# Moving a transpose, its eviction and the bias work to other places in the first stage of a three-stage graph network kernel

## The chip, the core and the metric

The kernel runs on one core of a Trainium2 chip. The metric is the device time of one execution in microseconds (us). Three executions of the kernel before took 1197.25, 1198.56 and 1198.85 us; the median is 1198.56.

## The reference, cut to what matters

Sixteen graphs ("batches" below) of 512 nodes with 128 features go through two layers. The first layer, which the change touches, is this:

```
def _gat(h, adj, W, a):                       # used twice, W1 a1 and W2 a2
    Wh = h @ W
    e = leaky_relu(Wh @ a[:128] + swapaxes(Wh @ a[128:], 1, 2), 0.2)
    att = softmax(where(adj > 0, e, -9e15), axis=1)
    return att @ Wh
h = layernorm(x + gat(gat(x)))                # "first norm"
x = layernorm(h + relu(h @ w_ff1 + b_ff1) @ w_ff2 + b_ff2)      # "second norm"
```

The second layer is attention with 8 heads whose values depend on the relation code of each edge (values `src @ Wv[r] + bv[r]`, r = 0 to 3), a norm, a feed-forward part and a norm. Its biases `bv` are what the bias work prepares.

## The kernel before, in words

The kernel has three stages: the graph layer (`graph_layer`, tiles named `a_...`, about the first 420 us), the attention (`b_...`) and the last feed-forward part (`c_...`). All sixteen inputs stay on the chip between them, in `xs` and `codes`.

A batch has 4 chunks (C) of 128 nodes (P) and is worked on in four successive steps. Step t, run by `step(t, begin, first, second, feed, more)` on each engine, does four things at once for four different batches:

- **begin**, batch t: transposes the features (`turn_x`, L499) into the PSUM bank `turn`, ScalarE copies them to `x_t` (L701), the adjacency codes are transposed (`turn_codes`, L531) and copied to `codes` (L708), `x_weights` multiplies by the weights (L541), and the first attention's row is spread (`spread_row(0, t)`, L555).
- **first**, batch t-1: the scores of the first attention. ScalarE makes `low` from the row (`lower`, L822), VectorE adds and leaks (L863, "leak") and masks with a minimum (L870, "mask"; the mask itself is made by `edges`, L1027), ScalarE takes exponentials (`exps`, L841), VectorE the reciprocal of the sums (`invert`, L897) and scales (L904), TensorE multiplies (`round_one`, L593), ScalarE copies the result (`keep_hw`, L809).
- **second**, batch t-2: the same for the second attention: `spread_row(1, ...)`, `lower`, leaks, masks, `exps`, `invert`. GpSimd scales by the reciprocal (`scale_hw`, L1064, writes `hw_n`), TensorE multiplies (`round_two`, L583), VectorE adds the input (`add_x`, L1040) and does the first norm: `norm_stats(0)` (L914 and L921), ScalarE's root `rstds(0)` (L847 and L854, a logarithm and an exponential), `norm_finish` (L928, four scalings).
- **feed**, batch t-3: TensorE transposes the normed features (`turn_h`, L506), ScalarE evicts them (`keep_h`, L802), then `feed_up` (L567), `hidden` on ScalarE (L835), `feed_down` (L573), `add_h` (L1033), `turn_y` (L513), the second norm `norm_stats(1)`, `rstds(1)`, `norm_shift` (L935, "shift"), `centre` (L829, four chunks on ScalarE), and `turn_n` (L519), which turns the normed batch back, and `keep_x` (L815), which writes it to `xs`.

Steps 0 to 3 are unrolled, steps 4 to 14 are a hardware loop, step 15 and a hand-written `tail` follow. The order on each engine is written out by hand in its `step` function, and each engine works strictly in that order, waiting on semaphores. `step` of TensorE is L597, of ScalarE L693, of VectorE L953, of GpSimd L1048. In a step GpSimd does two things: `scale_hw` and then `encode` (L461, four instructions at L467), which makes the codes of batch t+1 once VectorE's `see` (L943) has looked at the codes of batch t-1. In step 3 it also writes pads (`first_qk.pads`, L255 to L257).

The order of the row transposes, `turn_n` and `turn_x` at the joint of two steps on TensorE is, before the change, `spread_row(0, t)`, `turn_n(t - 3)`, `spread_row(1, t - 1)`, `turn_x(t + 1)`, `turn_h(t - 2)`. On ScalarE it is `exps`, `rstds(1)`, `centre`, `keep_hw`, `rstds(0)`, the copy of `s2` (L739), `keep_x`, then of the next step `lower(1)`, the copy of `x_t`, `lower(0)`, `keep_h`.

`keep_x` and `centre` have these waits:

```
def keep_x(b):
    act.wait_ge(n_turned, b + 1)
    act.wait_ge(summed[0], b + 1)
def centre(b):
    act.wait_ge(shift_ready, b + 1)
    act.wait_ge(n_turned, b)
```

`Preparation.vector_late` (L161) is called at the end of VectorE's step 1. It forms differences of the value weights and of the biases (3 rows of 512), and splits the biases into three bf16 parts, one to a row, in fourteen chained instructions and a last cast. Its scratch space is lent by `hid` and `y`. Ahead of it it waits for all late loads (`late_loaded`), for which every engine also waits ahead of step 2. The only user of the result, `first_qk.values`, is in the tail.

Of the kernel before, what the change touches and what calls it, by code (L numbers as in the profile page):

```python
# [49 lines left out]
class Preparation:  # L50
# [3 lines left out]
    def __init__(self, nc, z, w, io, keep, sb, banks, lent):  # L54
# [11 lines left out]
        self.rest, self.acc, self.part, self.part2 = [at[0:3, 0:NB] for at in lent]  # L66
# [94 lines left out]
    def vector_late(self, dve):  # L161

        D, R, w = self.z.D, self.z.R, self.w
        rows, rest, part, part2, acc = self.rows, self.rest, self.part, self.part2, self.acc
        count = [0]

        def then(ins):

            count[0] += 1
            ins.then_inc(self.chain, 1)  # L170
            dve.wait_ge(self.chain, count[0])

        dve.wait_ge(self.late_loaded, 16 * len(self.late_loads))
        dve.wait_ge(self.ident_made, 4)

        for r in range(1, R):
            then(dve.tensor_tensor(w["wv"][:, r, :], w["wv"][:, r, :], w["wv"][:, 0, :], ALU.subtract))
            then(dve.tensor_tensor(rows[:, r * D:(r + 1) * D], rows[:, r * D:(r + 1) * D],
                                   rows[:, 0:D], ALU.subtract))

        e = w["ident"]
        then(dve.tensor_copy(part[:, :], rows[:, :]))
        then(dve.tensor_tensor(rest[:, :], rows[:, :], part[:, :], ALU.subtract))
        then(dve.tensor_scalar(acc[:, :], part[:, :], e[0:3, 0:1], None, ALU.mult))
        then(dve.tensor_copy(part[:, :], rest[:, :]))
        then(dve.tensor_tensor(part2[:, :], rest[:, :], part[:, :], ALU.subtract))
        then(dve.scalar_tensor_tensor(out=acc[:, :], in0=part[:, :], scalar=e[0:3, 1:2], in1=acc[:, :],
                                      op0=ALU.mult, op1=ALU.add))
        then(dve.scalar_tensor_tensor(out=acc[:, :], in0=part2[:, :], scalar=e[0:3, 2:3], in1=acc[:, :],
                                      op0=ALU.mult, op1=ALU.add))  # L190
        dve.wait_ge(self.ident_made, 5)
        dve.tensor_copy(w["bias3"][0:3, :], acc[:, :]).then_inc(self.biases_split, 1)
# [166 lines left out]
def graph_layer(nc, z, w, io, xs, codes, other, general, flagged, shared, first_qk, sem_b, keep):  # L359
# [5 lines left out]
    with ExitStack() as ctx:  # L365
# [125 lines left out]
        def _(pe):  # L491
# [105 lines left out]
            def step(t, begin, first, second, feed, more):  # L597
                if second:
                    spread_row(1, t - 2)
# [1281 lines left out]
```

## Time and profile before

| | us |
|---|---|
| runs | 1197.25, 1198.56, 1198.85 |
| median | 1198.56 |
| profiled execution | 1198.38 |
| its span in the trace | 1196.6 |
| TensorE busy (matmuls) | 1076.5 (90%) |
| VectorE busy | 948.1 (79%) |
| ScalarE busy | 741.5 (62%) |
| GpSimd busy | 602.8 (50%) |

The span is from the first to the last instruction; 1.8 us of the profiled execution lie around it. The profile names the engines PE (TensorE), PEld (its weight loads), DVE (VectorE), ACT (ScalarE), POOL (GpSimd) and SP. A row of a timeline has the start and the duration in us, the engine, the line, the operation, what it writes and reads, and how many instructions were merged into the row; an end in brackets says how long the engine stood idle ahead of it and what released it. Where instructions overlap in the engine's pipeline, one starts a little before the one ahead has ended, and a merged row's duration is that of all of them. The granted clock is a share of TensorE's full 2.4 GHz; 0.50 is its lower level, 1.2 GHz.

### The profile page before, as it was taken

The page shows a single profiled execution, that of the slowest core. Times are in us where ns is not written, and L with a number is a line of the kernel's source. Part 1 is how long each engine was busy: PE and PEld are TensorE (multiplying, and loading weights), DVE is VectorE, ACT ScalarE, POOL GpSimd, SP SyncE. Part 2 cuts the span into 40 slices and gives each one's busy share as a digit, 9 for nine tenths or more (in the row PEclk, how much of TensorE's full clock was granted, in tenths as well). Part 3 has the DMA queues.
Part 4 walks back from the last instruction along what each step waited for, and adds up shares of the span by engine and source line. Part 5 has one row for each costly group of instructions (what it writes and reads, how often), then busy time and mean ns, then how long its engine had stood idle before and what let it go on. Part 6 is the DMA issues. An engine that isn't in the chain of part 4 may idle for free. (4 is left out here: it accounts for less than half of the span.)

```text
span 1196.6 us, 21640 instructions
## 1 busy us (share of the span) xinstructions
PE 1076.5 (90%) x6087; PEld 496.7 (42%) x6087; DVE 948.1 (79%) x2324; ACT 741.5 (62%) x1341; POOL 602.8 (50%) x513
## 2 busy tenths in 40 slices
PE   3488888988988779999999999999999999879996
PEld 3465665665664422323333233333333323234442
DVE  2878878878888758888888888888888888437777
ACT  3467778778777346666666666676666666544442
POOL 3231231231211158788788887888788877900000
PEclk8699999999999979999999999999999999989998
DMA  5312112112104143223321433134313420000000
GB/s 163 108 54 106 53 53 105 53 54 104 53 11 120 40 118 91 63 79 116 111 60 60 114 110 79 40 114 114 84 46 99 114 62 1 1 0 36 35 35 35
DMA packets 49545, 86.54 MB, mean 72 GB/s; under 512 B 8919, under 2 KB 35927, under 8 KB 44378
## 3 DMA queue, kind: packets, MB, share of 16 engines
q1 hardware_dynamic: 46586, 85.59, 23.3%
q10 hardware_dynamic: 2912, 0.40, 0.2%
q8 instruction: 20, 0.33, 0.1%
q14 instruction: 27, 0.22, 0.1%
HBM read 52.12 MB, written 29.36 MB: 68 GB/s over the span
## 5 line engine op out<-in xcount | busy, mean ns | idle before, releaser
L1489 DVE TENSOR_REDUCE top<-b_peak 128x1 f32<-128x512 f32 x488 | 327.8, 687 | 89.4 <-PE b_peak L1245 85.2
L1360 ACT ACTIVATE b_prob<-b_score 128x1024 f32<-128x1024 f32 x256 | 262.1, 1024 | 199.1 <-PE b_score L1260 197.2
L1622 POOL TENSOR_TENSOR b_picked<-b_prob,mask 128x512 f32<-128x512 f32 x192 | 236.2, 1257 | 61.7 <-ACT b_prob L1360 61.6
L1622 POOL TENSOR_TENSOR b_picked<-b_prob,b_mask 128x512 f32<-128x512 f32 x192 | 237.3, 1263 | 53.6 <-ACT b_prob L1360 53.6
L1064 POOL TENSOR_TENSOR a_hw_n<-a_hw,a_inv 128x512 f32<-128x512 f32 x16 | 16.7, 1041 | 211.8 <-DVE a_inv L897 198.9
L467 POOL TENSOR_SCALAR a_code<-a_adj_in 128x512 bf16<-128x512 int32 x64 | 72.0, 1125 | 82.9 <-DVE a_seen L943 55.0
L841 ACT ACTIVATE a_att<-a_att,a_least 128x512 f32<-128x512 f32 x128 | 90.9, 714 | 16.4 <-DVE a_least L870 16.4
L1245 PE MATMUL b_peak<-b_k_stack,b_q_stack 96*128 96x512 bf16 x256 | 98.3, 384 | 0.0
L1245 PE MATMUL b_peak<-shared 96*128 96x512 bf16 x232 | 89.9, 389 | 6.0 <-issue 6.0
L870 DVE CUSTOM_DVE_ANT_0 a_att<-a_att,a_no_edge 128x512 f32<-128x512 f32 x128 | 94.7, 758 | 0.0
L1739 ACT ACTIVATE c_hid<-c_mid,bff 128x512 f32<-128x512 f32 x64 | 44.0, 687 | 62.5 <-PE c_mid L1717 62.5
L1260 PE MATMUL b_score<-shared 98*128 98x512 bf16 x256 | 77.6, 384 | 0.0
L1260 PE MATMUL b_score<-b_q_stack,b_k_stack 98*128 98x512 bf16 x256 | 76.5, 380 | 0.0
L573 PE MATMUL a_out<-a_hid,wff 128*128 128x512 f32 x128 | 59.5, 605 | 18.5 <-ACT a_hid L835 18.5
L1286 PE MATMUL b_o_ps<-b_picked,b_dval 128*32 128x512 f32 x512 | 68.2, 604 | 7.7 <-DVE b_picked L1503 5.2
L583 PE MATMUL a_turn<-a_hw_n,a_att 128*128 128x128 f32 x512 | 62.7, 282 | 13.5 <-POOL a_hw_n L1064 13.5
L1286 PE MATMUL b_o_ps<-b_picked,dval 128*32 128x512 f32 x512 | 68.2, 604 | 5.0 <-DVE b_picked L1503 5.0
L583 PEld LDWEIGHTS a_turn<-a_hw_n,a_att 128*128 128x128 f32 x512 | 60.3, 197 | 25.4 <-issue 25.4
L1245 PEld LDWEIGHTS b_peak<-b_k_stack,b_q_stack 96*128 96x128 bf16 x256 | 24.6, 96 | 108.7 <-DVE top L1489 93.8
L1286 PE MATMUL b_o_ps<-b_prob,b_val 128*32 128x512 f32 x512 | 68.2, 604 | 0.3 <-ACT b_o_t L1371 0.3
L1286 PE MATMUL b_o_ps<-b_prob,val 128*32 128x512 f32 x512 | 68.2, 605 | 0.0
L593 PE MATMUL a_pair<-a_xw_n,a_att 128*128 128x130 f32 x512 | 62.4, 281 | 4.8 <-DVE a_xw_n L904 4.8
(216 smaller groups left out, 1952.3 us busy)
## 6 DMA issues: line engine op xcount, KB each, us to landing
a_adj_in<-in_adj SPq DMA_DIRECT2D x16, 1024.0 KB, 5.5
scratch<-shared SPq DMA_DIRECT2D x32, 384.0 KB, 2.7
shared<-scratch SPq DMA_DIRECT2D x16, 768.0 KB, 6.3
scratch<-shared SPq DMA_DIRECT2D x32, 256.0 KB, 3.0
b_q_stack<-scratch SPq DMA_DIRECT2D x8, 768.0 KB, 5.4
b_k_stack<-scratch SPq DMA_DIRECT2D x8, 768.0 KB, 8.1
a_x_in<-in_x SPq DMA_DIRECT2D x16, 256.0 KB, 2.6
xs<-in_x SPq DMA_DIRECT2D x16, 256.0 KB, 5.6
```

The source lines that it names most:

```text
L467: eng.tensor_scalar(code[:, c, :].rearrange("p (k q) -> p k q", k=C), adj_in[:, c, :].rearrange("p (q k) -> p k q", k=C), CODE_HI, CODE_LO ...
L573: mm = pe.matmul(out[:, :], w["wff2"][0][:, f, :], hid[:, f, :], start=(f == 0), stop=(f == FC - 1))
L583: mm = pe.matmul(turn[:, ic * D:(ic + 1) * D], att[1][:, jc, ic * P:(ic + 1) * P], hw_n[:, jc, :], start=(jc == 0), stop=(jc == C - 1))
L593: mm = pe.matmul(pair[:, ic // 2, at:at + D + 2], att[0][:, jc, ic * P:(ic + 1) * P], xw_n[:, jc, :], start=(jc == 0), stop=(jc == C - 1))
L841: act.activation(att[k][:, c, :], att[k][:, c, :], ACT.Exp, bias=least[k][:, c:c + 1], scale=-1.0, accum_out=total[k][:, c:c + 1]).then_in ...
L870: dve.tensor_tensor_reduce(att[k][:, c, :], att[k][:, c, :], no_edge[:, c, :], 1.0, HIGHEST, ALU.add, ALU.min, least[k][:, c:c + 1]).then_ ...
L1245: pe.matmul(peak[hh % 2][:, :], q_stack[par][0:K, h, c * P:(c + 1) * P], k_stack[par][0:K, h, :], start=True, stop=True).then_inc(sem("pea ...
L1260: mm = pe.matmul(score[u][:, k, :], k_stack[par][:, h, c * P:(c + 1) * P], q_stack[par][:, h, :], start=True, stop=True)
L1286: mm = pe.matmul(o_ps[32 * hh:32 * hh + 32, :], v[:, c, GH * g + hh, :], src[:, hh, :], start=(c == 0 and rel is None), stop=(c == C - 1 a ...
L1360: act.activation(prob[s % 2][:, 2 * u:2 * u + 2, :], score[u][:, :, :], ACT.Exp, scale=float(DH) ** -0.5).then_inc(sem("exp_ready"), 1)
L1489: dve.tensor_reduce(top[g][:, hh, c:c + 1], peak[hh % 2][:, :], AX.X, ALU.max, negate=True).then_inc(sem("peak_read"), 1)
L1622: pool.tensor_tensor(picked[(NR * s + rel) % 2][:, hh, :], prob[s % 2][:, hh, :], m, ALU.mult).then_inc(sem("picked_pool"), 1)
```

## The change

It does four things.

1. The bias work moves from VectorE's step 1 (`vector_late`) to GpSimd's step 3, behind the pads (`pool_late`). It has seventeen instructions there, each waiting for the one before, on tiles of its own, and multiplies by a broadcast column of the identity where VectorE used a scalar operand.
2. `turn_n` of a batch, and `keep_x`, its eviction, go one step on: on TensorE behind `spread_row(1, t - 2)` and ahead of `turn_x(t)`, on ScalarE behind the copy of `x_t` and ahead of `lower(0, t - 1)`. The tail follows suit.
3. On ScalarE the copy of `s2` goes ahead of the second norm's root, and `centre` does chunks 0 to 2 ahead of `keep_hw` and chunk 3 behind the first norm's root.
4. On VectorE `norm_shift` of the second norm goes behind `add_x`.

```diff
-        self.rest, self.acc, self.part, self.part2 = [at[0:3, 0:NB] for at in lent]
+        self.rest, self.acc, self.part = sb("rest", [3, NB]), sb("acc", [3, NB]), sb("part", [3, NB], BF16)
...
-    def vector_late(self, dve):
+    def pool_late(self, pool):
...
+        pool.wait_ge(self.late_loaded, 16 * len(self.late_loads))
 
         for r in range(1, R):
+            then(pool.tensor_tensor(w["wv"][:, r, :], w["wv"][:, r, :], w["wv"][:, 0, :], ALU.subtract))
+            then(pool.tensor_tensor(rows[:, r * D:(r + 1) * D], rows[:, r * D:(r + 1) * D],
+                                    rows[:, 0:D], ALU.subtract))
+        def row(k):
+            return w["ident"][0:3, k:k + 1].to_broadcast([3, R * D])
+
+        then(pool.tensor_copy(part[:, :], rows[:, :]))
+        then(pool.tensor_tensor(acc[:, :], part[:, :], row(0), ALU.mult))
+        for k in (1, 2):
+            then(pool.tensor_tensor(rows[:, :], rows[:, :], part[:, :], ALU.subtract))
+            then(pool.tensor_copy(part[:, :], rows[:, :]))
+            then(pool.tensor_tensor(rest[:, :], part[:, :], row(k), ALU.mult))
+            then(pool.tensor_tensor(acc[:, :], acc[:, :], rest[:, :], ALU.add))
+        pool.tensor_copy(w["bias3"][0:3, :], acc[:, :]).then_inc(self.biases_split, 1)
...
@@ -597,6 +594,8 @@ TensorE, step
             def step(t, begin, first, second, feed, more):
                 if second:
                     spread_row(1, t - 2)
+                if feed and not (isinstance(t, int) and t == 3):
+                    turn_n(t - 4)
                 if begin:
                     turn_x(t)
...
                 if begin:
                     spread_row(0, t)
-                if feed:
-                    turn_n(t - 3)
...
@@ -631,6 +628,7 @@ TensorE, tail
             def tail():
 
                 spread_row(1, B - 2)
+                turn_n(B - 4)
                 turn_h(B - 3)
...
                 first_qk.product(pe, row[0][:, :], 1, 0)
+
+                spread_row(1, B - 1)
                 turn_n(B - 3)
-
-                spread_row(1, B - 1)
...
@@ -699,6 +697,8 @@ ScalarE, step
                     act.copy(x_t[:, :], turn[:, :]).then_inc(x_t_ready, 1)
+                if feed and not (isinstance(t, int) and t == 3):
+                    keep_x(t - 4)
                 if first:
                     lower(0, t - 1)
...
-                if feed:
-                    rstds(1, t - 3)
-                    centre(t - 3)
-                if first:
-                    keep_hw(t - 1)
-                if second:
-                    rstds(0, t - 2)
                 if begin:
                     act.wait_ge(xw_ready, t + 1)
                     act.wait_ge(leaked[0], C * t)
                     act.copy(s2_own[:, :], xw[:, t, :, D + 2]).then_inc(s2_ready, 1)
                 if feed:
-                    keep_x(t - 3)
+                    rstds(1, t - 3)
+                    centre(t - 3, (0, 1, 2))
+                if first:
+                    keep_hw(t - 1)
+                if second:
+                    rstds(0, t - 2)
+                if feed:
+                    centre(t - 3, (3,))
...
@@ -743,6 +743,7 @@ ScalarE, tail
                 lower(1, B - 2)
+                keep_x(B - 4)
                 lower(0, B - 1)
...
@@ -964,13 +965,13 @@ VectorE, step
                 if feed:
                     norm_stats(1, t - 3)
+                if second:
+                    add_x(t - 2)
+                if feed:
                     norm_shift(t - 3)
                 if second:
-                    add_x(t - 2)
                     norm_stats(0, t - 2)
                     norm_finish(t - 2)
-                if isinstance(t, int) and t == 1:
-                    prep.vector_late(dve)
...
@@ -1056,6 +1057,7 @@ GpSimd, step
                 if isinstance(t, int) and t == 3:
                     first_qk.pads(pool)
+                    prep.pool_late(pool)
```

## Rows read from the trace of the kernel before

**Rows 1.** Busy time by stretch: us, busy by engine (instructions), granted clock, DMA share, GB/s

```profile
46.30:55.20 8.90, 0.01 (x1) 0.00 (x0) 8.79 (x19) 5.22 (x14) 1.04 (x1) 0.50 0.13 49
55.20:60.70 5.50, 5.46 (x32) 5.49 (x33) 2.71 (x10) 1.52 (x4) 1.48 (x2) 0.65 0.00 0
...
240.00:270.00 30.00, 26.36 (x195) 20.60 (x193) 24.26 (x79) 22.59 (x53) 9.68 (x9) 1.00 0.19 63
```

**Rows 2.** Timeline of TensorE in a looped step

```profile
266.55 0.65 PE L555 MATMUL a_row<-ident,a_hw 128*128 128x128 f32 x4
267.03 0.60 PE L499 MATMUL a_turn<-ident,a_x_in 128*128 128x128 f32 x4
268.60 0.65 PE L506 MATMUL a_out<-ident,a_y 128*128 128x128 f32 x4 [0.96 <-DVE a_y L928]
...
280.30 3.81 PE L583 MATMUL a_turn<-a_hw_n,a_att 128*128 128x128 f32 x32 [0.28 <-POOL a_hw_n L1064]
```

**Rows 3.** Timeline of ScalarE in the same step

```profile
265.81 0.60 ACT L809 COPY a_hw<-a_pair 128x520 f32<-128x520 f32 x1
266.66 0.30 ACT L847 ACTIVATE a_lnv<-a_mv,eps 128x4 f32<-128x4 f32 x1 [0.24 <-DVE a_mv L921]
266.99 0.21 ACT L854 ACTIVATE a_rstd<-a_lnv 128x4 f32<-128x4 f32 x1
...
267.34 0.78 ACT L815 ACTIVATE xs<-a_mid,columns 128x512 f32 x1
268.02 0.59 ACT L822 ACTIVATE a_low<-a_row 128x512 f32<-128x512 f32 x1
268.50 0.59 ACT L701 COPY a_x_t<-a_turn 128x512 f32<-128x512 f32 x1
...
269.45 0.80 ACT L802 ACTIVATE a_h_t<-a_out,columns 128x512 f32<-128x512 f32 x1
...
278.19 0.20 ACT L841 ACTIVATION_READ_ACCUMULATOR a_att<-a_att,a_least 128x1 f32 x1
```

**Rows 4.** Timeline of VectorE in the same step

```profile
263.25 0.38 DVE L921 BATCH_NORM_AGGREGATE a_mv<-a_stats 128x2 f32<-128x6 f32 x4 [0.15 <-DVE a_stats L914]
264.23 0.16 DVE L935 SCALAR_TENSOR_TENSOR a_shift<-a_mv,a_rstd 128x4 f32<-128x4 f32 x1 [0.60 <-ACT a_rstd L854]
264.51 0.69 DVE L1040 TENSOR_TENSOR a_y<-a_turn,xs 128x512 f32<-128x512 f32 x1
...
269.03 1.41 DVE L863 SCALAR_TENSOR_TENSOR a_att<-a_row,a_hw,a_low 128x512 f32<-128x512 f32 x2 [0.57 <-ACT a_low L822]
...
278.68 0.17 DVE L897 RECIPROCAL a_inv<-a_total 128x4 f32<-128x4 f32 x1
```

**Rows 5.** Timeline of GpSimd in steps 3 and 4 and in a looped step

```profile
87.28 0.53 POOL L257 MEMSET dval<- 128x512 f32 x1
100.20 1.04 POOL L1064 TENSOR_TENSOR a_hw_n<-a_hw,a_inv 128x512 f32<-128x512 f32 x1 [12.39 <-DVE a_inv L897]
...
264.41 1.12 POOL L467 TENSOR_SCALAR a_code<-a_adj_in 128x512 bf16<-128x512 int32 x1
...
279.11 1.04 POOL L1064 TENSOR_TENSOR a_hw_n<-a_hw,a_inv 128x512 f32<-128x512 f32 x1 [12.38 <-DVE a_inv L897]
```

**Rows 6.** VectorE: the shift of step 3 (timeline); the masks by line, min/median/max ns

```profile
84.55 1.02 DVE L935 SCALAR_TENSOR_TENSOR a_shift<-a_mv,a_rstd 128x4 f32<-128x4 f32 x1 [0.60 <-ACT a_rstd L854]
...
L870 DVE CUSTOM_DVE_ANT_0 a_att<-a_att,a_no_edge x128: 670/680/1633, 21.2 to 385.4; 128x512 f32<-128x512 f32 x128
```

**Rows 7.** Timeline of ScalarE and VectorE at the start of step 2

```profile
41.33 0.60 ACT L822 ACTIVATE a_low<-a_row 128x512 f32<-128x512 f32 x1
...
44.10 1.39 DVE L863 SCALAR_TENSOR_TENSOR a_att<-a_row,a_hw,a_low 128x512 f32<-128x512 f32 x2
```

**Rows 8.** By line, min/median/max ns: centring on ScalarE, a bf16-mixed subtraction on GpSimd

```profile
L829 ACT ACTIVATE a_y<-a_mid,a_shift,a_rstd x64: 449/457/465, 85.6 to 419.1; 128x128 f32<-128x128 f32 x64
...
L1628 POOL TENSOR_TENSOR shared<-shared x28: 1155/1162/1173, 439.8 to 950.9; 128x512 bf16<-128x512 f32 x28
```

More of the change, by code:

```diff
@@ L50, with __init__ @@
 class Preparation:
-    def __init__(self, nc, z, w, io, keep, sb, banks, lent):
+    def __init__(self, nc, z, w, io, keep, sb, banks):
         def sem(name):
@@ L159, in vector @@
         dve.memset(self.w["eps"][:, :], LN_EPS).then_inc(self.consts_made, 1)
-    def vector_late(self, dve):
+    def pool_late(self, pool):
         D, R, w = self.z.D, self.z.R, self.w
-        rows, rest, part, part2, acc = self.rows, self.rest, self.part, self.part2, self.acc
+        rows, rest, part, acc = self.rows, self.rest, self.part, self.acc
         count = [0]
@@ L170, in then @@
             ins.then_inc(self.chain, 1)
-            dve.wait_ge(self.chain, count[0])
-        dve.wait_ge(self.late_loaded, 16 * len(self.late_loads))
-        dve.wait_ge(self.ident_made, 4)
+            pool.wait_ge(self.chain, count[0])
+        pool.wait_ge(self.late_loaded, 16 * len(self.late_loads))
         for r in range(1, R):
[L177 to L192, printed above, removed]
+            then(pool.tensor_tensor(w["wv"][:, r, :], w["wv"][:, r, :], w["wv"][:, 0, :], ALU.subtract))
[11 more added lines that the diff above has]
+        pool.tensor_copy(w["bias3"][0:3, :], acc[:, :]).then_inc(self.biases_split, 1)
 class FirstQueries:
@@ L440, in graph_layer @@
         ff_done = sem("ff_done")
-        lent = [hid[:, 2 * k:2 * k + 2, :].rearrange("p f n -> p (f n)") for k in range(2)] + [
-            y[k][:, :, :].rearrange("p c d -> p (c d)").bitcast(BF16) for k in range(2)]
-        prep = Preparation(nc, z, w, io, keep, sb, mid + row, lent)
+        prep = Preparation(nc, z, w, io, keep, sb, mid + row)
         ctx.enter_context(nc.allow_non_contiguous_dma(reason="a few hundred values, once"))
@@ L822, in lower, with centre @@
                 act.mul(low[k][:, :], row[k][:, :], LEAK).then_inc(low_ready[k], 1)
-            def centre(b):
+            def centre(b, chunks=range(4)):
                 act.wait_ge(shift_ready, b + 1)
                 act.wait_ge(n_turned, b)
-                for c in range(C):
+                for c in chunks:
                     act.activation(y[1][:, c, :], mid[0][:, c * P:(c + 1) * P], ACT.Identity, bias=shift[:, c:c + 1],
```

## The prediction

> **What bounds the kernel now.** The change touches only the first stage, so I read it in this order: busy time by stretch, then the timeline of one steady step on each engine, then the places where the moved work has neighbours. In a steady stretch TensorE, VectorE and ScalarE are busy for 26.4, 24.3 and 22.6 of 30 us at full clock [rows 1]: nobody is idle for long, so the order on each engine sets the end. The eleven looped steps repeat every (279.11 - 100.20) / 8 = 22.36 us, by GpSimd's `scale_hw` product [rows 5].
>
> One closed chain runs through a step. I measure from T, the start of the `keep_hw` copy (L809, 265.81) [rows 3]. T to the first leak on VectorE: 3.22 (269.03). Leak to the attention sums' reciprocal: 9.65 (278.68). From there GpSimd's product starts 0.43 later, takes 1.04, and `round_two` starts at 280.30 = T + 14.49 [rows 2, 4, 5]. `round_two`, `turn_y`, `round_one` bring the next T 7.87 later.
>
> A second chain is almost as long: T, the first norm's root, `keep_x`, `lower`, `x_t`, `lower`, then `keep_h` at 269.45 = T + 3.64; from there ScalarE works on to the end of the second attention's last exponential's accumulator read at 278.19 + 0.20 = 278.39 [rows 3]. VectorE reads it at 278.68 [rows 4]. So this chain has 0.3 us of slack, and whatever delays `keep_h` by more than that delays the step.
>
> **The change, part by part.**
>
> 1. Biases leave VectorE (step 1). Its late work ended just before the leak at 44.10, which waited for nothing, while the `lower` product it needs ended at 41.33 + 0.60 = 41.93 [rows 7]. With 0.3 for the release, the leak can start near 42.2: gain 1.9 us. The following chain of this step is VectorE's, and TensorE stands idle from 46.3 to 55.2 waiting for it [rows 1], so I take the whole 1.9. Bounds: 0 and 2.2. The waits for the late loads stay; all engines have them ahead of step 2 anyway.
>
> 2. Biases on GpSimd (after the pads of step 3). GpSimd ends the pads at 87.28 + 0.53 = 87.81 and is wanted again at 100.20: 12.4 us [rows 5]. Added are 17 chained instructions: 6 of 128 columns, 4 casts, 3 products and 2 subtractions with a bf16 input, 2 additions, of 512 columns each. No row shows GpSimd on 3 partitions, a product with a broadcast column, or such a chain; I price by columns alone, from its 128-partition rows. Bf16-mixed, 512 columns: 1.16; f32: 1.04; casts between the memset's 0.53 and the encode's 1.12, taken 0.92, nearer the encode, which reads as well as writes; 128 columns: a quarter and overhead, 0.32; a link of the chain 0.1 (0.05 to 0.2) [rows 5, 8]. Sum 1.9 + 3.7 + 5.8 + 2.1 + 1.7 = 15.2 us (12.3 at the lowest prices, 18.2 at the highest). That alone is past the 12.4.
>
> Besides, the two engines hold each other up. A `shift` of 0.16 us took 1.02 at 84.55, beside GpSimd's encode, and a mask, 0.68 in the median, up to 1.63 [rows 4, 6]. From 88 to 102 VectorE has about seven masks (two SBUF inputs, 0.61 each), an `edges` and the four scalings of the first norm. Letting each wait for the GpSimd instruction in progress, and GpSimd for it, I worked the two lists through side by side: GpSimd ends at 107.0 (104.4 with the lowest prices, 109.3 with the highest). The product that waits behind it in GpSimd's queue then starts at 107.0 instead of 100.20: **+6.8 us** (4.2 to 9.1). TensorE's `round_two` waits for it, everything behind waits for that, and step 4 has no slack to give it back.
>
> The Trainium skill (SBUF — State Buffer, section Who interferes with whom) says the port pair that VectorE and GpSimd share is an exclusive lock held for an instruction. The trace agrees, by the 1.02 us against 0.16. A bandwidth shared in halves would put GpSimd's end about 2 us earlier, as a tiny instruction would then hardly be stretched.
>
> 3. TensorE's clock. It then stands idle some 6 us. The one like place is 46.3 to 55.2: TensorE idle, granted 0.50 (the 1.2 GHz level), and the next 5.50 us at 0.65. The 32 products of `round_two` there took 5.46 us against 3.81 at full clock [rows 1, 2]: +1.65, rounded up to 1.8 for what of the cold stretch lies behind them (0 to 2.4).
>
> 4. `turn_n` and `keep_x` one step on, `centre` split, `shift` behind `add_x`, s2's copy moved up. Steps 4 to 15.
>  - VectorE no longer idles 0.60 for the root ahead of `shift`; `add_x` goes there [rows 4]. The first norm's sums are ready some 0.5 earlier, so its root starts at the end of `keep_hw`, T + 0.60 instead of T + 0.85 [rows 3]. Three centred chunks instead of four precede T, but `keep_hw` also waits for `round_one`, and both came together before: T gains nothing.
>  - Root T + 0.60, second activation T + 0.93, chunk 3 of the centring T + 1.10 to T + 1.56 (0.46 for one, by the group of L829 [rows 8]). First `lower` T + 1.45 to T + 2.04, and VectorE's leak 0.42 behind it, T + 2.46 instead of T + 3.22. This is the intended gain, 0.76 us.
>  - TensorE: the row transposes start at T + 0.74 and let the next begin at T + 1.22 [rows 2]. `turn_n` now stands next and wants chunk 3: T + 1.60. `turn_x` is queued behind it: T + 2.08 to T + 2.68. Before it started at T + 1.22.
>  - ScalarE's next work after `lower` is the copy of `x_t`, which needs `turn_x`: T + 2.72, so ScalarE idles from T + 1.93 for **0.8 us** it did not idle before. Behind it are queued `keep_x` (0.68, from T + 3.19), `lower` (0.49), and `keep_h` at T + 4.36 instead of T + 3.64 [rows 3].
>  - `keep_h` is 0.72 later and its chain had 0.29 of slack, of which 0.01 is the release: each step is **0.44 us** longer, and what VectorE gained turns into a longer wait for the exponentials. Bounds: 0.1 (if `turn_n` need not wait for chunk 3) and 0.55. `turn_h` moves little (T + 2.56 against T + 2.79) and is hidden.
>  Eleven steps, 5 to 15, by 0.44: **+4.8 us**. Step 4's own share is inside the wait for GpSimd.
>
> 5. The rest: the moved s2 copy (0.17 of the 0.35 between second activation and `keep_x` [rows 3]) lies in ScalarE's idle time ahead of the second norm's root; with that cover gone it would cost its 0.17. No DMA is moved; the x load leaves with `turn_x`, under 1 us later with a step to spare. In the tail `keep_x` has no `x_t` ahead of it: 0.
>
> Sum: -1.9 + 6.8 + 1.8 + 4.8 = +11.5. The profiled execution took 1198.38 (span 1196.6), 0.2 under the runs' median 1198.56: **1209.9 us**.
>
> **The rivals.**
>
> A. `shift` falls into a GpSimd instruction. Today it runs at 264.23, ahead of the third encode at 264.41 [rows 4, 5]. Behind `add_x`, which can start at about 263.73 (0.1 after the sums' end at 263.25 + 0.38) and holds the engine 0.61 (its 0.69 less the overlap of 0.08), it comes at about 264.34. That is 0.07 us from an instruction that would keep it to 264.41 + 1.12 = 265.53, as in the step of 84.55 [rows 6]. The centring, then `keep_hw`, would be 0.85 late in some twelve steps: +10.2, 1220.1 us. Against it: those 0.07 us. The skill's page has the lock go to whoever starts first, which is what makes this sharp; a fair share would cost 0.1 a step.
>
> B. GpSimd's work fits. At the lowest prices 12.3 us against 12.4, if VectorE's collisions cost nothing and the clock holds: -1.9 + 4.8, 1201.3 us. Against it: the collisions [rows 6].
>
> C. Faster. GpSimd fits, and ScalarE does not wait for `x_t`: TensorE would have to end `turn_x` by T + 1.9 instead of T + 2.68. Then the leak's 0.76 counts up to the 0.3 of slack, -3.3 in eleven steps, and the 1.9 at the start: 1193.2 us. It decides from the point where chunk 3 and two sets of transposes are through before ScalarE ends `lower`. For it: TensorE idles 0.96 ahead of `turn_h`, so it has room [rows 2]. Against it: the order.
>
> D. Step 1's 1.9 us does not come, because something else holds step 2: 1211.8, inside the range.
>
> **How the numbers follow.** Forecast (with D) 0.50, A 0.24, B 0.14, C 0.12. The likeliest gives 1210. Its own range, by the bounds of items 1 to 4, is about 1203 to 1215; below it B, above it A lie, and to leave out 2 in 10 the range is 1201 to 1221. About 0.2% is what a measurement of this kernel can tell from no change. C is faster (0.11, the rest of it within), a low B is within 0.2% (0.05 together), all else slower: 0.84.
>
> **What would show it.** GpSimd: 17 instructions from about 86, ending near 105, and the `hw_n` product there some 5 us late; VectorE's masks beside them at over 1 us. ScalarE: idle of 0.8 ahead of `x_t`, released by TensorE's `turn_x`; the period of the looped steps 22.8. `shift` at 0.16 us in most steps (A: about 1 us, period 23.6). The granted clock below 1 near 100 to 110. VectorE's first leak of step 2 near 42.2. A period under 22.36 or a product that is on time would make the prediction wrong.

## The result and the profile after

The changed kernel takes 1204.97 us (median of five executions, 1203.67 to 1205.47) against 1198.85 (five, 1197.25 to 1199.32): ratio 1.0053, 95% interval 1.0041 to 1.0065. The medians differ by 6.1 us; the ratio stands for 6.4 us, with an uncertainty of about 1.4. Forecast were 1210 and a range of 1201 to 1221. The profiled execution took 1204.25 (span 1202.4), which stands 5.8 above the span of before, 1196.6; the readings below explain those 5.8.

**Start, and the wait for GpSimd.** Timeline of VectorE and TensorE, kernel after (start us, us, engine line operation; in brackets the idle time before it and what ended it):

```profile
41.33 1.41 DVE L864 SCALAR_TENSOR_TENSOR a_att<-a_row,a_hw,a_low 128x512 f32<-128x512 f32 x2 [7.74 <-PE a_row L552]
...
82.68 1.02 DVE L936 SCALAR_TENSOR_TENSOR a_shift<-a_mv,a_rstd 128x4 f32<-128x4 f32 x1
...
85.96 2.08 DVE L929 TENSOR_SCALAR a_y<-a_y,a_mv,a_rstd 128x128 f32<-128x128 f32 x4 [0.96 <-ACT a_rstd L855]
...
101.78 1.74 DVE L871 CUSTOM_DVE_ANT_0 a_att<-a_att,a_no_edge 128x512 f32<-128x512 f32 x1
...
52.48 6.53 PE L580 MATMUL a_turn<-a_hw_n,a_att 128*128 128x128 f32 x32 [6.83 <-POOL a_hw_n L1066]
...
105.13 5.84 PE L580 MATMUL a_turn<-a_hw_n,a_att 128*128 128x128 f32 x32 [5.52 <-POOL a_hw_n L1066]
```

The leak of step 2 starts at 41.33 instead of 44.10 [rows 7]. `shift` in step 3 still takes 1.02 [rows 6]. `norm_finish` (85.96) takes 2.08 where its four scalings take 1.12 in a looped step, and the last mask 1.74. `round_two` of step 4 waits 5.52 us for GpSimd and then takes 5.84 instead of 3.81 [rows 2]. GpSimd's timeline there:

```profile
85.92 0.46 POOL L176 TENSOR_TENSOR wv<-wv 128x128 f32<-128x128 f32 x1
...
89.08 0.60 POOL L184 CAST a_part<-a_rows 3x512 bf16<-3x512 f32 x1
...
95.23 2.14 POOL L190 TENSOR_TENSOR a_acc<-a_acc,a_rest 3x512 f32<-3x512 f32 x1
...
103.03 0.95 POOL L191 CAST bias<-a_acc 3x512 bf16<-3x512 f32 x1
103.95 1.03 POOL L1066 TENSOR_TENSOR a_hw_n<-a_hw,a_inv 128x512 f32<-128x512 f32 x1
```

The bias chain runs from 85.92 to 103.98, 18.06 us, and the product `hw_n` behind it starts at 103.95 instead of 100.20 [rows 5]. The clock, by stretch (us, busy by engine, granted clock):

```profile
100.00:102.00 2.00, 0.00 (x0) 0.00 (x0) 2.00 (x4) 0.69 (x3) 1.84 (x3) 1.00 0.00 0
102.00:104.00 2.00, 0.00 (x0) 0.00 (x0) 2.00 (x3) 1.15 (x3) 1.94 (x3) 0.64 0.00 0
104.00:108.00 4.00, 2.87 (x13) 2.90 (x14) 1.89 (x7) 0.46 (x3) 2.33 (x3) 0.50 0.00 0
108.00:110.00 2.00, 2.00 (x14) 2.00 (x13) 0.00 (x0) 0.00 (x0) 1.92 (x2) 0.65 0.00 0
```

TensorE idles, and the granted clock falls to 0.50 (the 1.2 GHz level) and is back at about 109.4, as the 0.65 between 108 and 110 says: `round_two` runs its first 4.2 us at half the clock.

**A looped step.** ScalarE, then TensorE, VectorE and GpSimd, kernel after; T is 295.14, the start of `keep_hw`:

```profile
295.14 0.59 ACT L810 COPY a_hw<-a_pair 128x520 f32<-128x520 f32 x1 [0.21 <-PE a_pair L590]
295.63 0.30 ACT L848 ACTIVATE a_lnv<-a_mv,eps 128x4 f32<-128x4 f32 x1
295.96 0.20 ACT L855 ACTIVATE a_rstd<-a_lnv 128x4 f32<-128x4 f32 x1
296.07 0.44 ACT L830 ACTIVATE a_y<-a_mid,a_shift,a_rstd 128x128 f32<-128x128 f32 x1
296.63 0.60 ACT L823 ACTIVATE a_low<-a_row 128x512 f32<-128x512 f32 x1
297.69 0.59 ACT L699 COPY a_x_t<-a_turn 128x512 f32<-128x512 f32 x1 [0.47 <-PE a_turn L496]
298.18 0.78 ACT L816 ACTIVATE xs<-a_mid,columns 128x512 f32 x1
298.85 0.60 ACT L823 ACTIVATE a_low<-a_row 128x512 f32<-128x512 f32 x1
299.33 0.79 ACT L803 ACTIVATE a_h_t<-a_out,columns 128x512 f32<-128x512 f32 x1
...
296.56 0.66 PE L516 MATMUL a_mid<-ident,a_y 128*128 128x128 f32 x4
297.06 0.60 PE L496 MATMUL a_turn<-ident,a_x_in 128*128 128x128 f32 x4
...
293.58 0.16 DVE L936 SCALAR_TENSOR_TENSOR a_shift<-a_mv,a_rstd 128x4 f32<-128x4 f32 x1
...
297.53 1.41 DVE L864 SCALAR_TENSOR_TENSOR a_att<-a_row,a_hw,a_low 128x512 f32<-128x512 f32 x2
...
308.16 0.18 DVE L898 RECIPROCAL a_inv<-a_total 128x4 f32<-128x4 f32 x1 [0.90 <-ACT a_att L842]
...
286.09 1.04 POOL L1066 TENSOR_TENSOR a_hw_n<-a_hw,a_inv 128x512 f32<-128x512 f32 x1 [12.53 <-DVE a_inv L898]
...
308.60 1.04 POOL L1066 TENSOR_TENSOR a_hw_n<-a_hw,a_inv 128x512 f32<-128x512 f32 x1 [12.51 <-DVE a_inv L898]
```

Read against [rows 3] (T + x is x us behind T): the root starts at T + 0.49, the fourth chunk is centred at T + 0.93, ScalarE idles 0.47 for TensorE's `turn_x` ahead of `x_t`, and `keep_h` comes at T + 4.19 instead of T + 3.64. The leak is earlier, T + 2.39 instead of T + 3.22, but the reciprocal now waits 0.90 for ScalarE's exponential where before it waited for nothing [rows 4]. `shift` takes 0.16. The period is 308.60 - 286.09 = 22.51 us, 0.15 over 22.36.

**Where the 5.8 us arise.** The start of the product `hw_n` in each step, after minus before in us, and what the forecast's terms give:

| | step 2 | step 3 | step 4 | step 5 | step 15 | tail, first | tail, second | second stage starts | end |
|---|---|---|---|---|---|---|---|---|---|
| measured | -2.75 | -1.87 | +3.75 | +5.93 | +7.78 | +6.94 | +7.06 | +5.65 | +5.8 |
| forecast | -1.9 | -1.9 | +4.9 | +7.1 | +11.5 | +11.5 | +11.5 | +11.5 | +11.5 |

### The profile page after: what moved, and what is told of

Read it like the earlier page. It is cut to its first block and busy times, and to the rows that moved or that the text cites. A ratio compares the mean times of both kernels' runs of the same rounds, so it can differ in the third digit from the quotient of the medians.

```text
span 1202.4 us, 21676 instructions
## 1 busy us (share of the span) xinstructions
PE 1081.0 (90%) x6087; PEld 499.4 (42%) x6087; DVE 942.4 (78%) x2310; ACT 741.2 (62%) x1341; POOL 618.7 (51%) x530
## 5 line engine op out<-in xcount | busy, mean ns | idle before, releaser
L871 DVE CUSTOM_DVE_ANT_0 a_att<-a_att,a_no_edge 128x512 f32<-128x512 f32 x128 | 97.5, 780 | 0.0
L580 PE MATMUL a_turn<-a_hw_n,a_att 128*128 128x128 f32 x512 | 65.6, 290 | 13.3 <-POOL a_hw_n L1066 13.2
L564 PE MATMUL a_mid<-a_h_t,wff 128*128 128x512 f32 x128 | 62.0, 606 | 13.6 <-ACT a_h_t L803 13.6
L580 PEld LDWEIGHTS a_turn<-a_hw_n,a_att 128*128 128x128 f32 x512 | 63.2, 205 | 25.2 <-issue 25.2
```

The source lines that it names most:

```text
L564: pe.matmul(mid[f % 2][:, :], w["wff1"][0][:, f * P:(f + 1) * P], h_t[:, :], start=True, stop=True).then_inc(mid_done, 1)
L580: mm = pe.matmul(turn[:, ic * D:(ic + 1) * D], att[1][:, jc, ic * P:(ic + 1) * P], hw_n[:, jc, :], start=(jc == 0), stop=(jc == C - 1))
L871: dve.tensor_tensor_reduce(att[k][:, c, :], att[k][:, c, :], no_edge[:, c, :], 1.0, HIGHEST, ALU.add, ALU.min, least[k][:, c:c + 1]).then_ ...
```

## The experiments

The sign and the amount of each difference below are against the kernel before, run beside that version (medians 1198.4 to 1198.5), where nothing else is said. The theory was the forecast's: GpSimd's late product and the cold clock behind it, and ScalarE's chain, which an ill-placed `turn_x` makes longer. The rivals are named with each run. "The order" is all of the change but the bias part.

**The two parts alone.** `bias_only` is the kernel before with `pool_late` on GpSimd in step 3:

```diff
-                if isinstance(t, int) and t == 1:
-                    prep.vector_late(dve)
...
+                    prep.pool_late(pool)
```

> The bias work on GpSimd's step 3, all else as before. Theory (the loss is the wait for GpSimd and the clock behind it): step 2 gains 1.9 us, the product of step 4 stands 3.7 to 4 us later than before by the trace (5.6 net of the gain), and the cold stretch behind it costs 2 more: +5.7 us in all, less 1.2 if the short cold stretch that the kernel before has at 400 to 404 falls elsewhere. The looped steps keep their 22.36 us. Rival (the order of the steps is where the time goes): this kernel is within 2 us of the one before.

Measured: 1201.75 us, ratio 1.0034 (1.002 to 1.0047), +3.3, less than expected. Its product of step 4 stands 1.96 late instead of 3.7 to 4, in part since this profile was 1.6 us ahead of the one of before already at the first attention's reciprocal in step 1 (30.97 against 32.57), ahead of any bias work; and its looped steps are shorter, as below. `order_only` is the changed kernel with the bias work back on VectorE:

> The order of the change, the bias work left on VectorE. Theory: ScalarE idles 0.47 us ahead of the copy of x_t, keep_h comes 0.55 later and the looped steps take 22.51 instead of 22.36 us: +1.65 us over eleven steps, or +0.5 if the short cold stretch near 400 us goes. Rival 1 (the order is harmless or a gain, everything is lost in step 4): 22.36 us or less in a step, 0 to -3 us. Rival 2 (shift meets GpSimd's encode once the alignment is undisturbed by step 4): 23.3 us in a step, +10 us.

Measured: 1199.46 us, ratio 1.0008 (0.9999 to 1.0017), +1.0, which is not clear of no change; by the trace its period is 22.51, its ScalarE idles the same 0.47, and its `keep_h` comes at the same T + 4.19. So the bias part carries most of the loss, and the lengthened step is the order's. Together the parts cost 4.3, the change 6.4; part of the difference is a gain that `bias_only` has and the change has not: its looped steps take 22.23, 0.13 under before. ScalarE's `lower` and VectorE's first leak in one of its steps:

```profile
293.75 0.59 ACT L819 ACTIVATE a_low<-a_row 128x512 f32<-128x512 f32 x1
...
294.62 1.41 DVE L860 SCALAR_TENSOR_TENSOR a_att<-a_row,a_hw,a_low 128x512 f32<-128x512 f32 x2 [0.43 <-ACT a_low L819]
```

The leak starts 294.62 - (293.75 + 0.59) = 0.28 after the end of `lower`; before it was 269.03 - (268.02 + 0.59) = 0.42 [rows 3, 4]. Nobody forecast this; `pad_vector` below takes it up.

**The bias work where GpSimd is free for 21 us.** `bias_step15` is `bias_only` with `pool_late` at t == B - 1 instead of 3.

> The bias work on GpSimd as in bias_only, but in step 15, where GpSimd has no encode and stands idle some 20 us between two products. Theory (place, not engine, is what costs): the 1.9 us of step 2 stay gained and the 18 us fit: -1.9 us, with up to 1 us given back by masks that wait for GpSimd. Rival (GpSimd's instructions cost wherever they stand, as they hold up VectorE's masks): -1.9 plus 3 or more, slower than before.

Measured: 1197.3 us, ratio 0.9992 (0.9983 to 1.0), -1.2, and 4.5 under `bias_only`. The product of step 4 is 3.6 us earlier than in `bias_only`, that of step 5 6.1, that of step 15 still 6.1 (342.77 against 348.88): a late product is carried through undiminished, and step 3 was the wrong place. But the chain is not free in step 15 either, as the rival had it. It ends at 359.71, 10 us before GpSimd is wanted, and still the product there is late: it starts 26.91 us after the one before instead of 22.75. Of the 6.1 us against `bias_only` 1.6 are left there, and the profiled spans differ by 1.7; the other 2.8 of the medians' 4.5 no trace shows. VectorE, `bias_step15`:

```profile
350.36 0.80 DVE L932 SCALAR_TENSOR_TENSOR a_shift<-a_mv,a_rstd 128x4 f32<-128x4 f32 x1 [0.60 <-ACT a_rstd L851]
...
353.89 3.43 DVE L925 TENSOR_SCALAR a_y<-a_y,a_mv,a_rstd 128x128 f32<-128x128 f32 x4 [0.72 <-ACT a_rstd L851]
...
369.29 0.18 DVE L894 RECIPROCAL a_inv<-a_total 128x4 f32<-128x4 f32 x1 [1.69 <-ACT a_att L838]
```

`shift` takes 0.80 instead of 0.16 and `norm_finish` 3.43 instead of 1.11. Beside GpSimd's 16 us VectorE loses 2.7 by its next leak. By the next reciprocal it is 4.5, but that reciprocal waits 1.69 for ScalarE, where in the kernel before it waited for nothing. The other 1.8 come by way of TensorE, which waits for the late scalings and loses its clock, so that ScalarE waits for it 3.05 us ahead of `keep_h` and then 0.99, 0.96 and 0.65 (TensorE and the granted clock, `bias_step15`; the kernel before idled 1.21 there, at full clock, and `turn_h` took 0.66):

```profile
357.38 1.11 PE L503 MATMUL a_out<-ident,a_y 128*128 128x128 f32 x4 [3.49 <-DVE a_y L925]
...
358.00:362.00 4.00, 4.00 (x8) 1.92 (x7) 4.00 (x10) 1.52 (x3) 1.64 (x2) 0.50 0.01 4
```

Beside the same chain `add_x`, with one input in PSUM and one in SBUF, keeps its 0.68 and the norm's sums, with one input, their 0.87 to 0.88. The Trainium skill (SBUF — State Buffer, section Who interferes with whom) has VectorE and a GpSimd instruction that reads SBUF exclude each other where VectorE reads two SBUF inputs, as `shift` does, or where a `tensor_scalar`, as the scalings are, uses both pairs of ports, and not with a single SBUF input otherwise; the trace agrees in all four.

**Which wait makes the step longer.** `order_centre_whole` is `order_only` with all four chunks of the centring ahead of `keep_hw`:

> As order_only, but all four chunks of the centring ahead of keep_hw, so that turn_n waits for no chunk behind the root. Theory (turn_n standing ahead of turn_x is what delays the copy of x_t, its wait for chunk 3 is the smaller part): turn_n starts 0.16 earlier, the copy of x_t with it, but keep_hw is pushed back 0.1 by the fourth chunk; a step of 22.45 to 22.55 us, within 1 us of order_only. Rival (the wait for chunk 3 is the whole loss): 22.36 us or less, at least 1.6 us under order_only.

Measured: 1196.17 us, ratio 0.9983 (0.9974 to 0.9991), 3.3 under `order_only`; period 22.26. The expectation failed, and the numbers are the rival's: the wait for the fourth chunk was dearer than held. It is not the whole loss, as the next run shows. With the chunk out of the way ScalarE idles 0.47 for the row transposes and 0.19 ahead of `x_t`, and `keep_h` comes at T + 3.92. Two further orders, the first one swap from `order_only`, the second built on `order_centre_whole`:

```diff
 TensorE, step, order_x_first
+                if begin:
+                    turn_x(t)
                 if feed and not (isinstance(t, int) and t == 3):
                     turn_n(t - 4)
-                if begin:
-                    turn_x(t)
```

> The changed order with the biases still on VectorE, and TensorE's turn_x put ahead of turn_n. In the changed order a looped step takes 22.51 us and ScalarE idles 0.47 us ahead of the x_t copy, which waits for turn_x, which stands in TensorE's queue behind turn_n and its wait for the fourth centred chunk. Theory: ScalarE's chain from keep_hw to the last exponential sets this period, so that with turn_x first the 0.47 us goes, keep_h comes some 0.5 us earlier (T + 3.7 instead of T + 4.2) and the period falls to 22.0: 11 steps by 0.5, some 5.5 us under the order alone (1199.5), so about 1194, under the kernel before as well. Rival: VectorE's chain sets the period, or turn_n, now the later one, holds keep_x as long as the copy was held: period 22.4 to 22.5, 1199.

> The same, and further: turn_x ahead of the row transposes and x_t's copy ahead of the first lower, with all four chunks of the centring ahead of keep_hw. Theory: ScalarE then idles neither for turn_x (0.47 us, or 0.19 with the centring whole) nor for the row transposes (0.47 with the centring whole), keep_h comes at T + 3.2, and ScalarE's chain is shorter than VectorE's. From there VectorE's own chain (leak to the attention sums' reciprocal, 9.74 us without idle) sets the period: leak at T + 2.4 to 2.5, period 21.6 to 21.8, 11 steps by 0.6 to 0.75 under the 22.36 of before: 1189 to 1192 us. Rival, as above: a period over 22.2, because turn_n or turn_h comes too late for keep_x or keep_h.

Measured: `order_x_first` 1191.74 us, ratio 0.9946 (0.9932 to 0.996), period 21.94; `order_x_ahead` 1191.62 us, 0.9947 (0.9933 to 0.9961), period 21.95. ScalarE and VectorE in a step of `order_x_first`, T = 283.86:

```profile
285.35 0.60 ACT L826 ACTIVATE a_low<-a_row 128x512 f32<-128x512 f32 x1
285.85 0.58 ACT L702 COPY a_x_t<-a_turn 128x512 f32<-128x512 f32 x1
...
287.46 0.80 ACT L806 ACTIVATE a_h_t<-a_out,columns 128x512 f32<-128x512 f32 x1
...
296.31 0.18 DVE L901 RECIPROCAL a_inv<-a_total 128x4 f32<-128x4 f32 x1 [0.20 <-ACT a_att L845]
```

The idle time ahead of `x_t` is gone, `keep_h` is at T + 3.60, and the step is 0.57 shorter than in `order_only` by that one swap: the theory holds, and the rival (VectorE's chain, or a late `turn_n`) does not. The reciprocal still waits 0.20 for ScalarE, so ScalarE's chain still sets the step. In `order_x_ahead` (the copy of `x_t` ahead of `lower` on ScalarE too) it is VectorE's:

```profile
286.85 1.41 DVE L865 SCALAR_TENSOR_TENSOR a_att<-a_row,a_hw,a_low 128x512 f32<-128x512 f32 x2 [0.50 <-ACT a_low L824]
...
296.49 0.17 DVE L899 RECIPROCAL a_inv<-a_total 128x4 f32<-128x4 f32 x1
```

The reciprocal follows without idle time, `keep_h` is at T + 3.39, but `lower` is later, at 285.81, and the leak waits for it and starts 0.44 after its end. Both chains are now within 0.2 us of each other. The period expected here, 21.6 to 21.8, was too low because of that later `lower`.

| kernel | ScalarE idle ahead of `x_t` | `keep_h` | reciprocal waits for ScalarE | period |
|---|---|---|---|---|
| before | 0 | T + 3.64 | 0 | 22.36 |
| order_only, after | 0.47 | T + 4.19 | 0.77, 0.90 | 22.51 |
| order_centre_whole | 0.19 | T + 3.92 | 0.50 | 22.26 |
| order_x_first | 0 | T + 3.60 | 0.20 | 21.94 |
| order_x_ahead | 0.25, not for TensorE | T + 3.39 | 0 | 21.95 |

**The 0.13 us ahead of the leak.** The leak is the first work of a step on VectorE, so the loop's jump back lies just ahead of it. The bias work there is fourteen instructions with its last cast, one fewer than the description ahead of the forecast says.

> The kernel before with the biases on GpSimd at step 15, and 14 one-column memsets with their waits at the very start of VectorE's program, some 150 instructions and 20 us ahead of any work that they could delay. In every looped step, VectorE's first leak follows the end of ScalarE's lower by 0.42 to 0.43 us in kernels that have the 14 bias instructions on VectorE ahead of the loop, and by 0.28 to 0.31 in those that have not; the period of before is 22.36, with the biases off VectorE 22.23. Theory: what stands ahead of the loop in VectorE's program sets where the loop's code lies and so what the jump back costs. Then 0.42 comes back, with a period of 22.36, and the time is 11 by 0.13 = 1.4 us over the 1197.3 of the kernel without the memsets. Rival: it hangs on where the scratch rows lie in SBUF, or on the bias work itself; then 0.29, 22.23 and 1197.3.

Measured: the period is 22.37 and the gap 0.42, in all looped steps:

```profile
289.00 0.59 ACT L823 ACTIVATE a_low<-a_row 128x512 f32<-128x512 f32 x1
...
290.01 1.41 DVE L864 SCALAR_TENSOR_TENSOR a_att<-a_row,a_hw,a_low 128x512 f32<-128x512 f32 x2 [0.57 <-ACT a_low L823]
```

So the theory holds in the step as far as the place of the code goes: the bias work is gone from VectorE, the scratch rows lie where they lay in `bias_step15`, and 14 one-column memsets at the start of its program bring the 0.13 back. Outside the loop nothing changes: in step 3 the gap is 0.27 in the kernel before, in `bias_step15` and in `pad_vector`. But on the loop's first pass, which no jump back precedes, it is 0.69 in the kernel before and in `pad_vector` and 0.33 in `bias_step15` and `vector_split`. So the jump back is not all of it: entering the loop costs more too in the kernels where the gap is long. It is no matter of the mere amount of code either: `after_unrolled`, below, has a whole step more ahead of its loop and a gap of 0.29 to 0.30. Why the place matters, and where the loop's code has to lie, was not tried. The time, 1200.25 us (ratio 1.0019, 1.0009 to 1.0028), is 2.95 over `bias_step15` where 1.4 was expected. By the traces `pad_vector` is 1.4 us behind from the period, 1.7 in all at step 15, but only 0.65 at the tail's two products, as it loses less in step 15; then it has a cold stretch of TensorE between 402 and 408 that `bias_step15` has not, and is 2.1 behind at the second stage's start. The rest arises behind, in code that is the same. So the time does not confirm the 1.4; the period and the gap do.

**The bias work left on VectorE.** `vector_split` keeps ten instructions of `vector_late` in step 1 and puts four into the tail:

```diff
                 first_qk.remainder(dve, pair[:, 0, :], 1, 1)
+                prep.vector_late(dve, 1)
                 invert(1, B - 1)
+                prep.vector_late(dve, 2)
```

> The kernel before with the biases still on VectorE, but the last four of their 14 instructions moved to the tail, into VectorE's idle time around the last reciprocal (1.89 and 2.17 us idle, 1.5 and 1.2 us of work). Theory: in step 1 VectorE is then through at about 41.5 us, the leak of step 2 starts near 42.2 instead of 44.10, 1.9 us earlier, of which some 1.5 to 1.9 arrive at the end, and nothing is paid on GpSimd: 1196.6 to 1197 us with the period of before, 22.36; if four instructions fewer ahead of the loop change the jump back, 22.23 and 1195.3. Rival: the gain at the start does not reach the looped steps, as GpSimd or the clock give it back in steps 2 and 3: 1198.5.

Measured: 1194.8 us, ratio 0.9975 (0.9964 to 0.9986), -3.6, a little past the better of the two cases. VectorE's part in step 1 ends at 38.5 rather than 41.5, as this profile stands 1.2 us earlier already at step 1's reciprocal (31.40 against 32.57), which is not the edit's doing, and two of its 512-column instructions (0.42 and 0.68 instead of 1.35 and 1.47) are through before GpSimd's encode starts at 35.88. The leak of step 2 starts at 40.79, the product of step 4 at 97.29 (before: 100.20), and the period is 22.24 with a gap of 0.30. Four instructions fewer ahead of the loop do what fourteen fewer did.

**What the cold clock cost.** `after_unrolled` writes step 4 out ahead of the loop; `after_filled` adds to it:

```diff
+                if isinstance(t, int) and t == 4:
+                    for _ in range(48):
+                        pe.matmul(turn[:, 0:P], ident[:, :], ident[:, :], start=True, stop=True)
                 if second:
                     round_two(t - 2)
```

> The changed kernel with step 4 written out ahead of the loop instead of being the loop's first pass: the control for the next run. Expected: 1205.0 us within 1.5 us, and the same cold stretch in step 4: TensorE idle 5.5 us, its round_two 5.8 us instead of 3.8.

> The same, and in step 4 TensorE runs 48 matmuls of 128 columns, whose result nobody reads, into the bank that round_two is going to write, while it waits for GpSimd's late product. Theory (item 3 of the prediction): the 2.0 us that round_two of step 4 takes longer are the clock's, which the chip lowered while TensorE idled; with the filler the granted clock stays at 1.0 and round_two takes 3.8 us: 2 us under the control, 1203. Rival: round_two is slow because its inputs or the bank are contended for by the engines that catch up behind the wait; then it stays near 5.8 us, 1205. If the filler is still running when the product is ready, up to 2 us of the gain are given back.

Measured: `after_unrolled` 1205.49 us (ratio 1.0052, 1.0037 to 1.0068), as expected. `after_filled` 1217.14 us (1.0146, 1.0127 to 1.0165). TensorE in step 4, first of `after_unrolled`, then of `after_filled`:

```profile
105.64 5.83 PE L580 MATMUL a_turn<-a_hw_n,a_att 128*128 128x128 f32 x32 [5.67 <-POOL a_hw_n L1066]
```

```profile
100.36 10.88 PE L616 MATMUL a_turn<-ident 128*128 128x128 f32 x96
111.08 3.74 PE L580 MATMUL a_turn<-a_hw_n,a_att 128*128 128x128 f32 x32
...
104.00:110.00 6.00, 6.00 (x56) 6.00 (x56) 3.09 (x9) 0.90 (x3) 4.28 (x6) 1.00 0.01 3
```

Behind the filler the clock is granted in full and the same 32 products take 3.74 us instead of 5.83. That run alone does not rule contention out, as GpSimd is busy beside `round_two` for 4.3 us in the control and for 1.1 here. But the clock accounts for the whole: in the changed kernel 4.2 us at half the clock do 2.1 us of work, which is the 2.1 between 5.84 and 3.74. As a remedy it failed. The filler was mis-sized: each f32 matmul of 128 columns shows as two, 0.11 us each, so 48 took 10.88 us, 5 us past the product that was ready at 106.06. That puts the second stage's start 3.3 us behind the control (438.91 against 435.65). The other 8 us arise inside the second stage: between 440 and 460 TensorE is busy 15.1 us at a granted clock of 0.70, in the control 19.9 at 0.98. One stall stands out, between two matmuls of one group (TensorE, `after_filled`):

```profile
441.87 1.06 PE L1303 MATMUL b_misc<-xs,wq 128*128 128x512 f32 x1
447.83 1.01 PE L1303 MATMUL b_misc<-xs,wq 128*128 128x512 f32 x1 [4.90 <-issue]
```

In the control the same pair runs without a gap. The 4.90 us have no release in the profile, and why they are there was not found; behind them the clock is at its lower level until about 452, in the control until about 441.

**Two finds together.**

> Two finds together: the changed order with TensorE's turn_x ahead of turn_n (alone 1191.7), and the last four bias instructions in VectorE's idle time of the tail instead of in step 1 (alone 1194.8, of which some 1.3 us come from a cheaper jump back in VectorE's loop). Theory: with this order ScalarE's chain sets the period (21.94 us), so only the start and the tail of the second add: 1191.7 - 2.3 = 1189.4, period 21.94. Rival: VectorE's earlier leak does shorten the step, 21.8: 1188.

> As the last, with the order in which VectorE's chain sets the period (turn_x ahead of the row transposes, x_t's copy ahead of lower, all four chunks centred ahead of keep_hw; alone 1191.6 with a period of 21.95, its leak 0.43 us behind lower). Theory: four instructions fewer ahead of VectorE's loop make the jump back 0.13 us cheaper, as in the kernel of which this part comes, and here that counts in each step: period 21.82, 1191.6 - 3.6 = 1188.0 us. Rival: the place of the loop's code falls otherwise in this kernel, 21.95: 1189.3.

Measured: `best_v_first` 1190.04 us, ratio 0.9932 (0.9918 to 0.9945), period 21.94; `best_v_x_ahead` 1189.88 us, ratio 0.9929 (0.9915 to 0.9942), period 21.83. The periods are the two that the theory gave: the shorter gap ahead of the leak shortens the step only where VectorE's chain sets it. Both times are over the expected 1189.4 and 1188.0, the second by 1.9, so that its time is nearer to its rival's 1189.3 and only the period speaks for the theory. Up to step 15 `best_v_x_ahead` is 2.98 us ahead of `order_x_ahead`, at the second stage's start 1.66: the tail gives some back, as this profile has a cold stretch of TensorE there (391.4 to 395.4) that the other has not. Both versions beat the kernel before by about 8.5 us (0.7%) and the changed kernel by 15.

## Why the prediction was right, and what was mis-sized

The sign and the mechanisms were right; the sum was 5.0 us too high against the median, 5.7 by the profiled spans (+11.5 against +5.8). The three larger misses, in items 2, 4 and 5, all lie on the same side.

1. **Bias off VectorE: -1.9 forecast, -1.87 measured** by the product of step 3. That they agree is luck. The leak moved by 2.77, but `lower` ahead of it came 0.78 earlier in this profile (40.55 against 41.33), 0.67 of which were there at step 1's reciprocal, ahead of any bias work; over the kernels here that reciprocal starts anywhere from 30.97 to 32.83. The edit's own gain was 1.99. Then 0.9 went again, which the forecast had at nothing: `round_two` of step 2 now starts earlier in the cold stretch and takes 6.53 us instead of 5.64, as the full clock came back only 0.9 us earlier (at about 58.2 against 59.1).

2. **Bias on GpSimd: +6.8 forecast, 3.75 + 1.87 = +5.6 measured.** The chain took 18.06 us where the side-by-side working gave 19.2. Alone the estimate of 15.2 was near: in `bias_step15`, with fewer collisions, it takes 15.9. The items differ more than the sum: the six small ones cost 0.45 each, not 0.32, whether on 3 partitions or 128; the casts 0.60 or 0.95, not 0.92; the additions up to 2.14. Rival B (it fits) fell by those 18.06 us against 12.4; that a late product would be carried through undiminished is shown by `bias_step15` against `bias_only`.

3. **Clock: +1.8 forecast, +2.03 measured**, and the time at half the clock accounts for it. The 5.46 us read for step 2 were cut off by the end of the window at 60.70; the timeline has 5.64, so that the 1.65 should have been 1.83.

4. **Order: 0.44 a step forecast, 0.15 measured in the period.** This is the term that was mis-sized most: 4.8 us forecast for the eleven steps 5 to 15, 2.0 measured. Ten looped steps gave 0.15 each, and step 15, which stands outside the loop, gave 0.50 (22.47 from the product before it against 21.97), a difference that the forecast did not make. Its chain of causes was right link by link (`turn_n` waits for the fourth chunk, `turn_x` behind it, ScalarE idle, `keep_h` late, VectorE's gain spent on waiting for exponentials), and `order_x_first` proves the link that matters. Two sizes were off. The root was put at T + 0.60, the end of `keep_hw`; it starts at T + 0.49, ScalarE taking its next instruction 0.1 before the last one ends, and ScalarE idled 0.47, not 0.8, so `keep_h` moved by 0.55 instead of 0.72. And the second chain's slack was read as 0.29 at its end. It is 0.40: from `keep_h` to the reciprocal takes 8.83 us when ScalarE works through (308.16 - 299.33), and 269.45 + 8.83 = 278.28 is 0.40 ahead of 278.68. The missing 0.11 lay in a small wait inside the chain of before: the copy of the codes came 0.80 after `keep_h` (at 270.25) where after comes 0.66. A chain that is not critical hides idle time in its middle too. 0.55 - 0.40 = 0.15. `order_centre_whole`, which shifts `keep_h` by 0.28 only, falls under the period of before, as 0.28 is less than 0.40.

5. **Tail: 0 forecast, -2.1 measured.** From step 15 to the tail's first product the distance fell from 22.75 to 21.91. 0.48 of that is the order's, as `order_only` has 22.27: there is no `turn_x` and no `x_t` there, so it has its gain without its price. Nearly all of the rest comes with the bias part: GpSimd's product starts 0.37 behind the reciprocal instead of 0.73, as it does in all six kernels with the bias work on GpSimd (0.36 to 0.39), where the eight others have 0.73 to 0.75; why was not tested. Then, between 400 and 404, the kernel before has a cold stretch of TensorE that the changed one has not:

```profile
400.00:402.00 2.00, 1.79 (x7) 1.36 (x7) 2.00 (x4) 1.46 (x4) 0.00 (x0) 0.60 0.00 0
402.00:404.00 2.00, 2.00 (x4) 0.53 (x3) 0.12 (x1) 1.07 (x2) 0.00 (x0) 0.54 0.00 0
```

and in the changed kernel, in the work that stands there 7 us later:

```profile
407.00:409.00 2.00, 1.78 (x8) 0.82 (x8) 2.00 (x4) 1.92 (x5) 0.00 (x0) 1.00 0.00 0
```

Of the other twelve profiles `pad_vector` and `best_v_x_ahead` have it, 11 to 15 us behind the tail's second product as here; `bias_only`, `order_only`, `bias_step15` and the rest have the full clock there. So those 1.4 us (7.06 to 5.65) belong to the moment more than to the change; no run settles what starts it.

The five add up: -1.87 + 5.62 + 2.03 + 2.0 - 2.13 = 5.65 at the second stage's start.

Of the rivals, A (`shift` locked out by the encode in every step) did not come: `shift` is 0.16 in the loop. The encode also begins at another moment after the change, at 291.39 with `shift` at 293.58; its third chunk starts near 293.7, so the margin was again about 0.1 us. C needed `turn_x` by T + 1.9. It was not there in the change, and `order_x_first` makes the order's half of that rival true by one swap: `turn_x` ends at T + 1.81, and the kernel is 6.7 us faster than before.

## What to carry to other kernels

When an instruction with a wait moves ahead in an engine's queue, look at what stands behind it that did not need the wait: one swap behind it was worth 0.57 us a step here, more than the move itself. Slack of a second chain is measured from its own working time without idle, not from its end. And work that one of VectorE and GpSimd does in SBUF is not free because the engine is idle: 16 us of small work on GpSimd cost VectorE 2.7 us, and TensorE's clock made 4.5 of them, with GpSimd wanted only 10 us later, while four of the fourteen instructions in VectorE's own idle time cost the tail under 0.1 us (`vector_split`). Last, agreement of a term is worth looking behind: item 1 was right to 0.03 us by a gain that was not the edit's and a loss that nobody had forecast.

## What the runs showed of the hardware beyond this

- The first instruction of a loop pass on VectorE came 0.13 us later or sooner by what stands ahead of the loop in its program: 0.41 to 0.44 us from the end of `lower` to the leak in six kernels, 0.28 to 0.32 in the eight with 4 or 14 instructions fewer there (two of these with a whole step more). `pad_vector` against `bias_step15` shows it by fourteen memsets.
- GpSimd's subtraction of 128 columns took 0.45 us on 3 partitions as on 128, against VectorE's 0.28 for the same work, and its cast of 512 columns 0.60 or 0.95: line 188 took 0.95 in the changed kernel and 0.60 in `bias_step15`.
- TensorE had the full clock when it began to idle at 99.6 and half of it when `round_two` began at 105.13; with matmuls of no use in that gap (`after_filled`) `round_two` began at the full clock.
